# A scan of 512 steps: three state banks with the product one scan later, five shared banks in rotation, and sums of middle halves joined by DMAs

## The reference

```python
A = -jnp.exp(A_log)

def step(h, ts):
    dt_t, B_t, C_t, u_t = ts
    dA = jnp.exp(dt_t[..., None] * A)
    h = h * dA + (dt_t * u_t)[..., None] * B_t[:, None, :]
    y = jnp.einsum('bds,bs->bd', h, C_t)
    return (h, y)
...
y = ys.transpose(1, 0, 2) + xc * D
y = y * jax.nn.silu(z)
```

## Time and profile before

| | |
|---|---|
| Median of 3 runs | 1604.46 us (1599.95 to 1605.29) |
| The profiled execution | 1611.44 us, span 1609.6 us |
| TensorE busy | 1349.1 us (84%) |
| VectorE busy | 1258.5 us (78%) |
| GpSimd busy | 1164.6 us (72%) |
| ScalarE busy | 890.1 us (55%) |
| mean granted TensorE clock | 0.902 of full speed |
| first scan, last scan | start at 67.3 and 1528.1 us |

### The profile page before, as it was taken

One profiled execution on the slowest core, in us unless ns is written; L12 is line 12 of the kernel. 1 busy time (PEld: TensorE's weight loads), 2 busy tenths in 40 slices (PEclk: granted clock), 3 DMA queues, 4 the chain that ended last, 5 costly groups with the idle time before them and its releaser, 6 DMA issues.

```text
span 1609.6 us, 17492 instructions
## 1 busy us (share of the span) xinstructions
PE 1349.1 (84%) x5158; PEld 957.9 (60%) x5158; DVE 1258.5 (78%) x1571; ACT 890.1 (55%) x1948; POOL 1164.6 (72%) x590
## 2 busy tenths in 40 slices
PE   4874762988988998989998997899998998889977
PEld 2641211766676856766776666676776676646546
DVE  6689864778878986789887977889887987777734
ACT  4643352574756665576667565655756464545522
POOL 0535888867887778877896778776996789786730
PEclk8587766999999998999999998999998999979889
DMA  4774443655474637754474537464575457456540
GB/s 161 274 256 144 152 156 136 228 199 165 135 283 156 225 100 228 249 183 172 172 274 167 202 122 259 161 226 159 190 248 197 146 169 276 157 184 203 180 152 27
DMA packets 124607, 300.64 MB, mean 187 GB/s; under 512 B 14408, under 2 KB 29136, under 8 KB 114016
## 3 DMA queue, kind: packets, MB, share of 16 engines
q1 hardware_dynamic: 112224, 272.91, 49.9%
q0 software_dynamic: 6144, 16.79, 3.2%
q10 hardware_dynamic: 6144, 9.83, 1.7%
HBM read 259.75 MB, written 39.71 MB: 186 GB/s over the span
## 4 chain that ended last, share of the span: by engine, by line
PE 41%; DVE 14%; issue 13%; POOL 9%; ACT 8%; DMA 5%; SPq 1%; DVEq 0%; ACTq 0%; POOLq 0%
PE prod L944 33%; DVE state L1322 9%; DMA xs<-slot_x 4%; POOL dbu L681 4%; PE ysum L993 4%; POOL hxc L692 3%; DVE hxc L1290 2%; POOL slot_x L668 2%; PE prod L1128 1%; ACT state L752 1%; PE prod L949 1%; PE prod L1129 1%; ACT late L910 1%; DVE prod L1359 1%; DMA late<-slot_y,slots 1%
## 5 line engine op out<-in xcount | busy, mean ns | idle before, releaser
L1322 DVE TENSOR_TENSOR_SCAN state<-state,carry,dbu 128x512 f32<-128x512 f32 x512 | 657.7, 1285 | 179.1 <-ACT state L752 148.6
L681 POOL TENSOR_TENSOR dbu<-dtu,bb 128x1024 f32<-128x1024 f32 x256 | 608.1, 2383 | 67.3 <-DVE state L1322 58.4
L692 POOL TENSOR_TENSOR hxc<-hxc 128x1024 f32<-128x1024 f32 x155 | 366.5, 2364 | 223.9 <-DVE hxc L1290 223.9
L752 ACT ACTIVATE state<-dt,par 128x512 f32<-128x512 f32 x512 | 353.5, 692 | 94.3 <-DVE hxc L1290 78.1
L1290 DVE TENSOR_TENSOR hxc<-state,cb 128x512 f32<-128x512 f32 x512 | 353.7, 691 | 36.2 <-DVE state L1322 0.5
L944 PE MATMUL prod<-late 128*128 128x256 f32 x1136 | 281.6, 406 | 26.6 <-issue 17.0
L993 PE MATMUL ysum<-hxc,ident 128*128 128x512 f32 x404 | 224.8, 686 | 75.6 <-DVE hxc L1290 41.4
L944 PE MATMUL prod<-xsT,late 128*128 128x256 f32 (+1 forms) x1280 | 270.2, 365 | 15.7 <-DVE xc L1345 3.9
L944 PEld LDWEIGHTS prod<-late 128*128 128x128 f32 x1136 | 236.2, 211 | 71.2 <-issue 37.3
L944 PEld LDWEIGHTS prod<-xsT,late 128*128 128x128 f32 x1280 | 226.9, 196 | 68.8 <-issue 37.8
L750 ACT COPY carry<-state 128x1 f32<-128x1 f32 x384 | 61.1, 159 | 250.3 <-DVE hxc L1290 234.5
(11 more groups left out here) (164 smaller groups left out, 1216.7 us busy)
## 6 DMA issues: line engine op xcount, KB each, us to landing
bb<-bc_rows SPq DMA_DIRECT2D x256, 256.0 KB
cb<-bc_rows SPq DMA_DIRECT2D x256, 256.0 KB
late<-moe SPq DMA_DIRECT2D x40, 1028.0 KB, 4.9
late<-moe SPq DMA_DIRECT2D x40, 1024.0 KB, 5.8
slot_x<-xc SPq DMA_DIRECT2D x18, 512.0 KB, 5.7
xs<-slot_x SPq DMA_DIRECT2D x31, 256.0 KB, 6.1
slot_y<-ys ACTq DMA_DIRECT2D x31, 256.0 KB, 5.4
late<-x SPq DMA_DIRECT2D x12, 512.0 KB, 9.4
```

Of the source, the lines that this page charges most:

```text
L681: nc.gpsimd.tensor_tensor(dbu[:, v % 3, :, :], dtu[:, n % 2, 2 * h:2 * h + 2, :], b, ALU.mult).then_inc(dbu_ready, 1)
L692: nc.gpsimd.tensor_tensor(hxc[:, to, :, :], hxc[:, to, :, :], hxc[:, piece, :, :], ALU.add).then_inc(summed, 1)
L752: nc.scalar.activation(state[:, k % 2, :], dt[:, (2 * n + h) % 3, k % 2, :], ACT.Exp, scale=par[:, P_ALOG + col(k):P_ALOG + col(k) + 1]).t ...
L1322: nc.vector.tensor_tensor_scan(state[:, c, :], state[:, c, :], dbu[:, v % 3, c, :], carry[:, n % 2, col(k):col(k) + 1], ALU.mult, ALU.add) ...
```

## The change

- Three state banks. VectorE issues scan k and right behind it the product of step k - 1; `BETWEEN` and the list of what is owed are gone, and chores stand behind both. `decay(k + 1)` waits for the product of step k - 2.
- In blocks 1 to 6 a half is one chain of four groups of four. GpSimd still adds within a group. Behind the second, third and fourth group a LINK, a DMA issued by GpSimd with add on arrival, adds its sum in hxc to that of the first; it waits for the link before it. No matmul follows: YE reads the joined sum from hxc. Blocks 0 and 7 keep their sums on TensorE.
- hxc has seven buffers; the plan gives them back at other steps.
- No ysum: five banks in rotation, from which sums on TensorE take two per half.
- The A work of ScalarE comes two steps late instead of one.

```diff
@@ -47,8 +47,12 @@
 NK = NB * NS * DC
 NV = NK // 2
 BASE_STEP = NS * DC
-GROUPS = [((1,) * NS,) * 2] + [((4,) * 4,) * 2] * (NB - 2) + [((4,) * 3 + (1,) * 4, (2,) * 2 + (1,) * 12)]
-HX = 5
+ALONE = ((1,),)
+GROUPS = [(ALONE * NS,) * 2] + [(((4, 4, 4, 4),),) * 2] * (NB - 2) + [(((4,),) * 3 + ALONE * 4, ((2,),) * 2 + ALONE * 12)]
+HX = 7
+BANKS = 5
+STATES = 3
+MID_LATER = 0
 
 STEPS_A = {"LOADX": 0, "XR": 7, "TR0": 11, "TR1": 13, "XD": 40, "BOUT": 42, "DT0": 44, "DT1": 46, "DT2": 48, "DT3": 50,
...
-BETWEEN = ("CV", "YE", "OU", "M2")
-LATER = {"act": {"R": 1, "M": 1, "C": 1, "A": 1}, "dve": {"M": 1, "C": 1, "A": 0}, "pool": {"Y": 1, "A": 1},
+LATER = {"act": {"R": 1, "M": 1, "C": 1, "A": 2}, "dve": {"M": 1, "C": 1, "A": 0}, "pool": {"Y": 1, "A": 1},
...
+    units, groups, r = [], [], 0
     for n in range(NB):
-        for sizes in GROUPS[n]:
-            for size in sizes:
-                units += [(q, j, size) for j in range(size)]
-                q += 1
-    return units
-
-
-Y_UNIT = y_units()
-Y_GROUPS = Y_UNIT[-1][0] + 1
+        for chains in GROUPS[n]:
+            for chain in chains:
+                for place, size in enumerate(chain):
+                    units += [(len(groups), j, size) for j in range(size)]
+                    groups.append((r, place))
+                r += 1
+    return units, groups
+
+
+Y_UNIT, Y_CHAIN = y_units()
 LAST_UNIT = {q: v for v, (q, j, size) in enumerate(Y_UNIT)}
 FIRST_UNIT = {q: v for v, (q, j, size) in enumerate(Y_UNIT) if j == 0}
+LAST_GROUP = {r: q for q, (r, place) in enumerate(Y_CHAIN)}
+FIRST_GROUP = {r: q for q, (r, place) in enumerate(Y_CHAIN) if place == 0}
+WHOLE = [r for r in LAST_GROUP if LAST_UNIT[LAST_GROUP[r]] - FIRST_UNIT[FIRST_GROUP[r]] == NS - 1]
 
 
 def adds_before(v):
...
+            r, place = Y_CHAIN[q]
+            if place:
+                back.append((2 * v + 9, table[FIRST_UNIT[q]][0], ("linked", q)))
+            if q == LAST_GROUP[r]:
+                back.append((2 * v + (14 if place else 6), table[FIRST_UNIT[FIRST_GROUP[r]]][0], ("y_acc", accs_until(r)) if r not in WHOLE else
+                             ("y_whole", 2 * WHOLE.index(r) + 2)))
     return table
 
 
...
@@ -160,13 +183,17 @@
     for v in range(NV):
         if Y_UNIT[v][1]:
             out[2 * v + 1].append(("Y", "ADD", v))
-        if Y_UNIT[v][1] == Y_UNIT[v][2] - 1:
-            out[2 * v + 1].append(("Y", "ACC", Y_UNIT[v][0]))
+        q, j, n = Y_UNIT[v]
+        r, place = Y_CHAIN[q]
+        if j == n - 1 and place:
+            out[2 * v + 2].append(("Y", "LINK", q))
+        if j == n - 1 and q == LAST_GROUP[r] and r not in WHOLE:
+            out[2 * v + (6 if place else 1)].append(("Y", "ACC", r))
     for n in range(NB):
...
@@ -226,6 +253,8 @@
         return "dve", (kind, name, i)
     if kind == "M" and name == "DN0":
         return "act", (kind, "DN%d" % (size(i) - 1), i)
+    if kind == "Y":
+        return "dve", ("C", "YE%d" % (i % 2 * 2 + int(name[3])), i // 2)
...
+        elif kind == "Y" and name == "ACC" and FIRST_UNIT[FIRST_GROUP[i]] % NS == 0:
+            for c in range(2):
+                take(("Y", "SUM%d" % c, FIRST_UNIT[FIRST_GROUP[i]] // NS))
...
-        state = ctx.enter_context(nc.psum_tensor("state", [P, 2, BT], F32))
-        ysum = ctx.enter_context(nc.psum_tensor("ysum", [P, 2, BT], F32))
-        prod = ctx.enter_context(nc.psum_tensor("prod", [P, 4, BT], F32))
+        state = ctx.enter_context(nc.psum_tensor("state", [P, STATES, BT], F32))
+        prod = ctx.enter_context(nc.psum_tensor("prod", [P, BANKS, BT], F32))
...
 
             eng.wait_ge(xn_ready, (g + 1) * NT)
+
+        def group_added(eng, q):
+
+            if Y_CHAIN[q][1]:
+                eng.wait_ge(linked[Y_CHAIN[q][0] % 4], 16 * links_until(q))
+
+        def group_summed(eng, q):
+
+            if Y_UNIT[LAST_UNIT[q]][1]:
+                eng.wait_ge(summed, adds_before(LAST_UNIT[q]) + 1)
 
         def is_full(key):
             return full_[USES[key][0]], 1
...
+                elif kind == "Y" and name == "LINK":
+                    group_summed(pool, i)
+                    group_added(pool, i - 1)
+                    to, piece = (HX_OF[FIRST_UNIT[q]][0] for q in (FIRST_GROUP[Y_CHAIN[i][0]], i))
+                    pool.dma_start(flat3(hxc[:, to, :, :]), flat3(hxc[:, piece, :, :]), accum_op=ALU.add
+                                   ).then_inc(linked[Y_CHAIN[i][0] % 4], 16)
...
@@ -743,18 +793,20 @@
                     act.wait_ge(neg_a_ready, 2)
                 if k % 32 == 0:
                     act.wait_ge(dt_ready, 2 * n + h + 1)
-                if k >= 2:
-                    act.wait_ge(hc_ready, k - 1)
-                if 2 <= k < (NB - 2) * BASE_STEP + 2:
-                    b = (k - 2) // BASE_STEP % 2
-                    nc.scalar.copy(carry[:, b, col(k - 2):col(k - 2) + 1], state[:, k % 2, BT - 1:BT]).then_inc(carried, 1)
-                    act.wait_ge(carried, k - 1)
-                nc.scalar.activation(state[:, k % 2, :], dt[:, (2 * n + h) % 3, k % 2, :], ACT.Exp,
+                last = k - STATES
+                if last >= 0:
+                    act.wait_ge(hc_ready, last + 1)
+                if 0 <= last < (NB - 2) * BASE_STEP:
+                    b = last // BASE_STEP % 2
+                    nc.scalar.copy(carry[:, b, col(last):col(last) + 1], state[:, k % STATES, BT - 1:BT]).then_inc(carried, 1)
+                    act.wait_ge(carried, last + 1)
+                nc.scalar.activation(state[:, k % STATES, :], dt[:, (2 * n + h) % 3, k % 2, :], ACT.Exp,
                                      scale=par[:, P_ALOG + col(k):P_ALOG + col(k) + 1]).then_inc(decay_ready, 1)
 
...
                 elif kind == "Y" and name == "ACC":
-                    v = LAST_UNIT[i]
-                    first = FIRST_UNIT[i] % NS == 0
-                    if first and v >= NS:
-                        pe.wait_ge(y_free, 2 * (v // NS))
-                    if Y_UNIT[v][1]:
-                        pe.wait_ge(summed, adds_before(v) + 1)
+                    v, start = LAST_UNIT[LAST_GROUP[i]], FIRST_UNIT[FIRST_GROUP[i]]
+                    first = start % NS == 0
+                    sums = [("Y", "SUM%d" % c, v // NS) for c in range(2)]
+                    if first:
+                        free(pe, sums[0])
+                        free(pe, sums[1])
+                    if v > start:
+                        group_summed(pe, FIRST_GROUP[i])
+                        group_added(pe, LAST_GROUP[i])
                     else:
                         pe.wait_ge(hc_ready, 2 * v + 2)
                     for c in range(2):
-                        last = pe.matmul(ysum[:, c, :], ident[:, :], hxc[:, HX_OF[FIRST_UNIT[i]][0], c, :], start=first,
+                        last = pe.matmul(bank(sums[c]), ident[:, :], hxc[:, HX_OF[start][0], c, :], start=first,
                                          stop=v % NS == NS - 1)
                     last.then_inc(y_acc, 1)
...
@@ -1271,33 +1326,27 @@
                     dve.wait_ge(routed, 1)
                     dve.sem_inc(routed, 1)
 
-            owed = []
-
...
+            def product(k):
+
                 v, c = k // 2, k % 2
                 buf, what = HX_OF[v]
                 if c == 0:
                     dve.wait_ge(cb_in[v % 4], 16 * (v // 4) + 16)
                     if what and what[0] == "summed":
                         dve.wait_ge(summed, what[1])
+                    elif what and what[0] == "linked":
+                        group_added(dve, what[1])
+                    elif what and what[0] == "y_whole":
+                        dve.wait_ge(y_whole, what[1])
                     elif what:
                         dve.wait_ge(y_acc, what[1])
                 dve.wait_ge(scanned, k + 1)
-                nc.vector.tensor_tensor(hxc[:, buf, c, :], state[:, c, :], cb[:, v % 4, :],
+                nc.vector.tensor_tensor(hxc[:, buf, c, :], state[:, k % STATES, :], cb[:, v % 4, :],
                                         ALU.mult).then_inc(hc_ready, 1)
 
             def do(kind, name, i):
-                if kind == "S":
+                if kind in "SL" or name[:2] in VECTOR_WORK or name in ("M201", "M211"):
                     chore(kind, name, i)
-                elif kind == "L" or name[:2] in VECTOR_WORK or name in ("M201", "M211"):
-                    if name[:2] not in BETWEEN:
-                        product()
-                    chore(kind, name, i)
-                    product()
 
             def chore(kind, name, i):
                 if kind == "L":
...
@@ -1319,10 +1367,13 @@
                         dve.wait_ge(carried, (n - 1) * BASE_STEP)
                     dve.wait_ge(decay_ready, k + 1)
                     dve.wait_ge(dbu_ready, v + 1)
-                    nc.vector.tensor_tensor_scan(state[:, c, :], state[:, c, :], dbu[:, v % 3, c, :],
+                    nc.vector.tensor_tensor_scan(state[:, k % STATES, :], state[:, k % STATES, :], dbu[:, v % 3, c, :],
```

(24 more changed lines are left out.)

38 lines of the change are left out of this document (19 added, 19 removed).

## The result

The changed kernel takes 1591.24 us (median of six, 1584.85 to 1593.77), the kernel before 1602.61 beside it (six, 1599.95 to 1605.62): ratio 0.9923, interval 0.9902 to 0.9944. It is 11 to 12 us faster (9 to 16 by the interval), where 45 were forecast. The profiled execution took 1589.44 us, its span 1587.6.

What follows compares the result with a forecast made beforehand. TensorE, VectorE and GpSimd close together, none full. Blocks 1 to 6: -19 (VectorE's net -31 at 0.6), -24 matmuls, +6 links, -37; block 0 -6, block 7 -2: -45, 1560 us median. Forecast 1540 to 1580; wide range 1518 to 1604.

Steps and rivals of the forecast that it cites:

- Scan to product: VectorE, each step: product starts 1.19 us behind the scan, 0.18 saved a step, 55 us in blocks 1 to 6.
- The second rival: VectorE's wait on itself is worth nothing, the gap comes back before the next scan: 1600 us, chance 0.08.
- YE reads SBUF twice: 24 VectorE instructions in middle halves, two SBUF tensors beside GpSimd: 1.0 us each, 24 us, bounds 0 and 57.
- The sum without that term: Whole kernel: the forecast gain of 45 us without the 14 us charged for YE's two SBUF operands, 59 us.
- Sums off TensorE: Blocks 1 to 6: 192 matmul instructions, 96.6 us busy, go; gain taken as 24 us, between 0 and 96.6.
- A shift: ScalarE's A steps one step later: counted at nothing, bounds -10 and +10 us.
- Links: 36 DMAs issued by GpSimd, 1.26 us each, 45 us more on GpSimd: cost 6 us, between 0 and 45; landing free.
- The fifth bank: Blocks 1 to 6, five rotating banks replace four: 0 to -5 us, taken as 0.
- blocks 0 and 7: Block 0: -6 us from later products. Block 7: -3 for waits, +1 for banks, -2.
- Both reliefs in full: VectorE paces nearly everywhere, its waits shrink by 34 us, YE seldom meets GpSimd: about 1505 us, chance 0.13.
- GpSimd the bound: GpSimd's work grows to 887 us, in-order waits keep it from more than 84%: 1585 to 1600 us, chance 0.17.
- The late link: The last link of a half lands after YE and VectorE waits: slower, 1625 to 1660 us, chance 0.14.

Runs made afterwards that it cites:

- operand in PSUM: The changed kernel with YE of blocks 1 to 6 adding a state bank in PSUM instead of hxc, sum left out of the result: 1548.54 us, ratio 0.9683.
- the base without the stall: The changed kernel with xc * D made on ScalarE and joined by a fourth link, YE gone from blocks 1 to 6: 1543.23 us, ratio 0.962.
- the two kernels whose YE is not held up: The changed kernel with one YE operand in PSUM (1548.54 us, 0.9683), and with GpSimd waiting while YE runs (1550.9 us, 0.9673).
- GpSimd paused: The changed kernel with a wait in GpSimd's list, two steps ahead of YE's place, until YE of the half is done: 1550.9 us, ratio 0.9673.
- the kernels with YE free: The changed kernel with YE's operand in PSUM (0.9683), GpSimd waiting for YE (0.9673), xc * D joined by link (0.962), or middle YE left out (0.9599).

## Why the prediction was right or wrong

The direction was right, and 1591 is inside the wide range of 1518 to 1604. It is above the forecast's 1540 to 1580, and the gain was put four times too large. Step by step:

- **Scan to product.** Right: 1.19 us everywhere, from 1.32 and 1.42. With YE at its 0.74 us, VectorE's program is 1013.2 - 170.5 = 842.7 (operand in PSUM), 61 less than before; 55 were worked out. Its weight was put at 0.6. Measured in blocks 1 to 6 it is 0.4 to 0.5 (31 us of time for 66 of program, and 27 for 72 on the base without the stall, where the profiled execution was 9 us under its median; undoing it costs more program than 61, since no chore stands between scan and product there). Over the whole kernel it was to be 33 + 9 = 42, and is 37 without the stall, 28 beside it. The second rival falls with it. The Trainium skill, "VectorE: DVE Perf Modes" (The DRAIN you can't avoid), says of a chain of copies that a semaphore behind each costs nothing extra; the 1.42, the 1.32 and the 28 to 37 us disagree.
- **YE reads SBUF twice.** This step failed. The mechanism was read rightly from the earlier trace rows, but it was priced at half a GpSimd instruction, 1.0 us each, as if YE met it at a random moment. Measured: 1.70 each, 41 us in place of 24. In nine of the twelve pairs the price held: 20 us for 18 operations, 1.1 each, though not at random, for the first mostly slipped in ahead of GpSimd's add and the second waited for all of it. In the other three one operation was passed over by two or three further instructions (up to 8.52 us), which no term had: 21 us. The sum is within the bound of 57 which the prediction gave, and then did not use. The second part of the failure is the weight: 24 counted 0.6, 14 us. The runs give 38 to 43 (operand in PSUM) and 40 (GpSimd paused) for 41, so a weight of about one. An even 0.13 or 0.23 a step is at least half taken up by waits that shrink; a lump of 2 to 8 us is not. That this is the reason for one weight of 0.4 to 0.5 and another of 1 is argued from these rows, not tested by itself. 14 forecast, 38 to 43 measured: 24 to 29 of the 34 missing microseconds.
- **The sum without that term.** 45 + 14 = 59 us forecast; 51 and 52 measured in the two kernels whose YE is not held up (ratios 0.9683 and 0.9673). The rest of the sum therefore held within 8 us. That is in part luck, for its parts are off in both directions, the links most:
- **Sums off TensorE.** 24 forecast; 27 to 33 without the stall, 8 to 10 beside it. "TensorE busy near 858" was wrong, it is 899: 96.6 us of matmuls went, and 56 of busy time. Part of this is the subtraction, for the records overlap: without its sums TensorE covers 871 us in the kernel before, not 858. The other 27 us are matmuls that take longer. The largest group, of after and then of before:

```profile
L996 PE MATMUL prod<-late 128*128 128x256 f32 x1046 | 263.2, 412 | 35.9 <-issue 35.9
```

```profile
L944 PE MATMUL prod<-late 128*128 128x256 f32 x1031 | 252.9, 403 | 24.1 <-issue 14.9 <-ACT late L910 7.1 <-ACT xsT L918 0.9
```

  The granted clock fell from 0.95 to 0.93 and the engine stands more; with matmuls put back it rose to 0.96 and the others cover 18 us less. In proportion to the clock the steps would make some 20 of the 27 us and some 28 in place of the 18 (estimates from 871 and 881 us), so the clock is of the right size for both; no run changes it alone.
- **A shift.** Counted at nothing within 10. Undoing it cost 8 us, but with YE 10 us longer; so little is left for the shift itself, as forecast.
- **Links.** The issue took 0.81 us in place of 1.26, the landing 7.5 (at most 11.0) under a cover of 10 to 13, and VectorE waited 4.0 us for them in all. What they cost in all was put at 6. Late product and matmuls make 37 + 27 = 64 us, by the ratios 74, and the kernels with YE free are 51 to 64 under the one before; so links, buffers and the overlap of the two cost up to 23. The run with links of 64 KB allows up to some 20 for the traffic, which the prediction counted at nothing beside the 6 for the issue. The fifth bank, 0 to -5, is worth 0; blocks 0 and 7 lost 2.5 and 3.8 us for 6 and 2.
- **The rivals.** *Both reliefs in full*: no, VectorE's waits did not shrink (172.5 from 164.2). *GpSimd the bound*: much that speaks for it came, dbu waits from 4.1 to 18.7 us, the chain on GpSimd, and a time of 1591 inside its 1585 to 1600 (GpSimd was 83% busy, short of the 86% named as a sign). But with the same work on GpSimd and YE freed the kernel took 1551, with GpSimd at 85.6%, and 1543 at 87%, beyond the 84% that the rival took for a ceiling. *The late link*: no. A result in a rival's interval is not the rival's mechanism.

The Trainium skill, "SBUF — State Buffer" (two separate sides), has this contention as an exclusive lock: whichever of a GpSimd operation and a VectorE operation with two SBUF inputs starts first holds the pair for its whole length, and the other is fully blocked. The pairs at 727 and at 997 agree, the GpSimd instructions that were held included (2.79 to 2.84 us). The case at 812 doesn't: by that rule YE would start when the current instruction ends, and it was passed over three times, as at 637 (twice) and 1163 (three times).

## What to carry to other kernels

Before an operand of VectorE moves from PSUM to SBUF, count how many GpSimd instructions follow one another without a pause at that place, look whether their records overlap, and take that row as the bound of the price, not half of one instruction; then either keep one operand in PSUM, let another path do the addition, or let GpSimd wait for it. Weigh a delay by its shape: small even ones were half absorbed here, a lump counted in full. Don't subtract the busy time of a group of matmuls from TensorE's: count the others by themselves. Before a difference between two kernels is put down to the edit, compare the length of the stalled operation in both: it moved by 16 and 10 us under two edits that left YE alone. And when the chain of waits names an engine, test it with a kernel that leaves that engine's work as it is.
